# VectorE's order in the retention heads of a decoder layer: the value block's first sum and the sine product trade places

## The chip, the cores and the metric

One core of one Trainium2 chip runs the whole program. The metric is the device time of one execution in microseconds, from first to last instruction of the core, with what lies around them; the median of several runs counts.

## The reference, cut to what matters

The program is one decoder layer in float32 on 8 sequences of 100 tokens (800 columns): retention with 8 heads, cross attention to a context of 722 tokens, a gated feed-forward part, each followed by a sum with its input and a layer norm. The change lies in the retention alone:

```
q, k = rope(x @ Wq), rope(x @ Wk)          # per head 128 wide
v, g = x @ Wv, x @ Wg                      # per head 256 wide
scores = (q * scale) @ k.T * decay         # per batch and head
o = scores @ v
o = o * rsqrt(mean(o*o) + eps) * g_norm_weight * silu(g)
attn = o.reshape(B, T, H * DV) @ Wo
rope(x) = [x1*cos - x2*sin, x2*cos + x1*sin]
```

The inputs are float32, and the outputs keep that precision.

## The kernel before, in words

**Precision by splitting.** Each float32 operand is split into a high part in fp32r, which ScalarE copies, and a low part, which VectorE gets by subtracting the high part from the source. A product is three TensorE passes: high by high, high by low, low by high. So each 128x512 piece of weights costs one ScalarE instruction (`entry_hi`, L1726) and one VectorE subtraction (`entry_lo`, L1993) ahead of TensorE's use. A ring of four pieces holds them: ScalarE may write piece e only when TensorE has finished piece e - 4.

**The heads.** Head 0 and head 7 are written apart. Heads 1 to 6 run the function `head(i)`, once in each engine's program. A head has three blocks: block 0 is query and key, block 1 the two value tiles, block 2 the two gate tiles. A block is computed by a Strassen scheme: seven products p0 to p6 of 12 matmuls each (L2511, L2513, L2515; each 128x400), from four mixed weight pieces (`mix`, L2025) and mixed activations that are kept (SIDE). The sums of products are made by VectorE (`combine`, L2051) out of PSUM in the order u2, u3, c22, c21, c12, with one copy by ScalarE before them (`keep`) and one between (`first_quarter`, L1758). TensorE's product p3 of a block waits for the sum u2 of that block, p5 for u3, p6 for c22, since they write the PSUM banks that these sums read.

**The order of one head on TensorE**: seven products of block 0 (with the transposes of the head before between them), seven of block 1, the output projection of head i - 1 in eight tiles (`project_output`, L2372 to L2374), scores, transposes of the values, seven products of block 2. The eight tiles take turns in two pairs of PSUM banks, so tile n from the third on waits until VectorE has added tile n - 2 to R (`add_output`, L2114): `if n >= 2: pe.wait_ge(r_added, 8 * i + (n - 1 - 8))`.

**The rotation.** Query (n = 0) and key (n = 1) share the two scratch tiles T1 and T2. For each of them VectorE multiplies by the cosine into T1 (`rotate_cos`, L2093) and by the sine into T2 (`rotate_sin`, L2097). GpSimd waits for the sine product and issues two accumulating DMAs that add T2 with its halves exchanged to T1 (L1700), waits until both have landed, and raises `roped` (L1703). ScalarE then makes the high part (`rotated_hi`, L1784), VectorE the low part (`rotated_lo`, L2104), and only then may the cosine product of n = 1 write T1. VectorE's queue is in order: what stands behind `rotated_lo` waits with it.

**Weights.** SyncE loads 1 MB pairs of pieces (L1661). The load of block 2's pair is issued when the low part of block 1's last piece (p6) is made, that of the next head's first pair when the low part of the fourth output piece is made.

Every order here is written out by hand, in `head(i)` of `vector` and of `scalar`; nothing plans it. Lines touched: `head` in `vector` and `head` in `scalar`. Lines of helpers that the steps below pass: `combine` L2051, `mix` L2025, `entry_lo` L1993, `output_lo` L2164, `gated_output` L2174.

Of the kernel before, what the change touches and what calls it, by code (L numbers as in the profile page):

```python
# [1514 lines left out]
def phase_retention(c, nc, sem, before, norm):  # L1515


    with ExitStack() as ctx:
# [186 lines left out]
        def scalar(act):  # L1705
# [30 lines left out]
            def output_entry_hi(i, n):  # L1736
                pair = pair_of(i, 2)
                entry_hi(PER * (i - 1) + OUTPUT_ENTRY + n, raw_quarters(pair)[:, n, :], pair, None)
# [43 lines left out]
            def rotated_hi(i, n):  # L1782
                act.wait_ge(roped, 2 * i + (n + 1))
                act.activation(QK[n][0], T1, ACT.Copy).then_inc(qk_hi, 1)  # L1784
# [81 lines left out]
            def head(i):  # L1866

                if i > 1:
                    product_hi(i, 0, 3)
                    keep(i, 0)  # L1870
                product_hi(i, 0, 4)
                if i == 1:
                    side_hi(4)
                else:
                    act.preload_act_table_set("silu_and_others")
                    gates(i - 1)
                    act.preload_act_table_set("natural_log_exp_and_others")
                product_hi(i, 0, 5)
                product_hi(i, 0, 6)
                if i > 1:  # L1880
                    output_hi(i - 1)
                product_hi(i, 1, 0)
                first_quarter(i, 0)
                if i == 1:
                    output_hi(i - 1)
                product_hi(i, 1, 1)
                product_hi(i, 1, 2)

                product_hi(i, 1, 3)
                keep(i, 1)  # L1890
                product_hi(i, 1, 4)
                product_hi(i, 1, 5)
                product_hi(i, 1, 6)
                output_entry_hi(i, 0)
                rotated_hi(i, 0)
                output_entry_hi(i, 1)
                first_quarter(i, 1)
                output_entry_hi(i, 2)
                output_entry_hi(i, 3)
                rotated_hi(i, 1)  # L1900
                product_hi(i, 2, 0)
                product_hi(i, 2, 1)
                product_hi(i, 2, 2)
                product_hi(i, 2, 3)
                scores_hi(i)
                turned_hi(i)
                keep(i, 2)
                product_hi(i, 2, 4)
                product_hi(i, 2, 5)
                product_hi(i, 2, 6)  # L1910
                token_squares(i, 0)
                if i < STRASSEN:
                    product_hi(i + 1, 0, 0)
                token_squares(i, 1)
                if i < STRASSEN:
                    product_hi(i + 1, 0, 1)
                else:
                    u = U_END_HEAD
                    act.wait_ge(c.raw[(u // 2) % 2], raw_count(u // 2))
                    act.wait_ge(f_done, F_DONE + LAST_ENTRY - 1)  # L1920
                    act.activation(c.WH[:, u % 2, :], raw_unit(c, u), ACT.Copy).then_inc(c.w_hi, 1)
                root(i)
                if i == STRASSEN:
                    act.wait_ge(x_back, X_BACK + 16)
                    act.wait_ge(f_done, F_DONE + LAST_ENTRY)
                    act.activation(operand(0, 1)[0], F1, ACT.Copy).then_inc(t_hi, 1)
                scaled_rows(i)
                if i < STRASSEN:
                    product_hi(i + 1, 0, 2)
# [45 lines left out]
        def vector(dve):  # L1975
# [30 lines left out]
            def mix(i, j, n):  # L2006

                pair, m = pair_of(i, PAIR[j]), block(i, j)
                raw = raw_quarters(pair)
                if n == 0:  # L2010
                    dve.wait_ge(c.raw[pair % 2], raw_count(pair))
                    if m > 0:
                        dve.wait_ge(f_lo, F_LO + entry(i - (j == 0), (j - 1) % 3, 3) + 1)
                    out, x, y, op = S3[:], raw[:, 0, :], raw[:, 2, :], ALU.subtract
                elif n == 1:
                    out, x, y, op = raw[:, 2, :], raw[:, 2, :], raw[:, 3, :], ALU.add
                elif n == 2:
                    dve.wait_ge(f_lo, F_LO + entry(i, j, 0) + 1)
                    out, x, y, op = raw[:, 0, :], raw[:, 2, :], raw[:, 0, :], ALU.subtract
                else:  # L2020
                    dve.wait_ge(f_lo, F_LO + entry(i, j, 4) + 1)
                    out, x, y, op = raw[:, 1, :], raw[:, 1, :], raw[:, 0, :], ALU.subtract
                if n:
                    dve.wait_ge(s_op, S_OP + 4 * m + n)
                dve.tensor_tensor(out, x, y, op).then_inc(s_op, 1)  # L2025
# [178 lines left out]
            def head(i):  # L2204
                if i > 1:
                    combine(i - 1, 2, "c12")
                    product_lo(i, 0, 2)
                    product_lo(i, 0, 3)
                    product_lo(i, 0, 4)
                    mix(i, 0, 3)  # L2210
                    combine(i, 0, "u2")
                    gated_output(i - 1)
                    product_lo(i, 0, 5)
                    combine(i, 0, "u3")
                    combine(i, 0, "c22")
                    mix(i, 1, 0)
                    mix(i, 1, 1)
                    product_lo(i, 0, 6)
                else:
                    combine(i, 0, "u2")  # L2220
                    product_lo(i, 0, 4)
                    mix(i, 0, 3)
                    side_lo(4)
                    product_lo(i, 0, 5)
                    combine(i, 0, "u3")
                    combine(i, 0, "c22")
                    product_lo(i, 0, 6)
                    mix(i, 1, 0)
                    gated_output(i - 1)
                product_lo(i, 1, 0)  # L2230
                if i == 1:
                    mix(i, 1, 1)
                mix(i, 1, 2)
                product_lo(i, 1, 1)
                output_lo(i - 1, 0)
                combine(i, 0, "c21")
                output_lo(i - 1, 1)
                product_lo(i, 1, 2)

                combine(i, 0, "c12")  # L2240
                product_lo(i, 1, 3)
                rotate_cos(i, 0)
                product_lo(i, 1, 4)
                rotate_sin(i, 0)
                mix(i, 1, 3)
                combine(i, 1, "u2")
                product_lo(i, 1, 5)
                combine(i, 1, "u3")
                combine(i, 1, "c22")
                product_lo(i, 1, 6)  # L2250
                output_entry_lo(i, 0)
                rotated_lo(i, 0)
                rotate_cos(i, 1)
                rotate_sin(i, 1)
                output_entry_lo(i, 1)
                combine(i, 1, "c21")
                output_entry_lo(i, 2)
                add_output(0, i)
                combine(i, 1, "c12")

                output_entry_lo(i, 3)
                add_output(1, i)
                mix(i, 2, 0)
                add_output(2, i)
                rotated_lo(i, 1)
                product_lo(i, 2, 0)
                add_output(3, i)
                mix(i, 2, 1)
                add_output(4, i)
                mix(i, 2, 2)  # L2270
                product_lo(i, 2, 1)
                add_output(5, i)
                product_lo(i, 2, 2)
                add_output(6, i)
                add_output(7, i)
                product_lo(i, 2, 3)
                mask_scores(i)
                scores_lo(i)
                turned_low(i)

                product_lo(i, 2, 4)
                combine(i, 2, "u2")
                mix(i, 2, 3)
                product_lo(i, 2, 5)
                product_lo(i, 2, 6)
                combine(i, 2, "u3")
                combine(i, 2, "c22")
                if i < STRASSEN:
                    mix(i + 1, 0, 0)
                    mix(i + 1, 0, 1)  # L2290
                    product_lo(i + 1, 0, 0)
                    mix(i + 1, 0, 2)
                    product_lo(i + 1, 0, 1)
                else:
                    plain_lo(U_END_HEAD)
                combine(i, 2, "c21")
# [2150 lines left out]
```

## Time and profile before

| what | value |
|---|---|
| median of 3 runs | 2631.72 us (2630.65 to 2632.12) |
| profiled execution, its own time | 2630.63 us |
| its span, first to last instruction | 2628.8 us |
| TensorE busy (matmul) | 2593.5 us, 99% |
| VectorE busy | 1814.5 us, 69% |
| ScalarE busy | 1197.4 us, 46% |
| heads 1 to 6 | about 548 to 988 us of the span |

The heads 2 to 6 are 72.5 us each. A matmul's busy time is longer than the distance to the next one (0.34 against 0.18 us), since they are pipelined; so a hole in TensorE's work is read from the starts of neighbouring matmuls. The granted TensorE clock was full throughout (0.999 over the span).

### The profile page before, as it was taken

To read this page: it belongs to the slowest core of one execution; us is meant where nothing else is said; L and a number is where in the kernel's file an instruction comes from. 1 tells how busy PE (TensorE), PEld (TensorE's weight loads), DVE (VectorE), ACT (ScalarE), POOL (GpSimd) and SP (SyncE) were. 2 spreads that over 40 slices of the span, in tenths; PEclk is the share of its full clock that TensorE was granted. 3 is DMA by queue.
4 is the path that set the end of the run, shared out by engine and by line. 5 is a ranking of instruction groups with operands and counts; after the bars stand their busy time and mean duration, and the time that the engine had idled before them with its cause. 6 is when DMAs were issued, how large, how long until landed. Compare 5 with 4: busy or idle time off the path is not lost.

```text
span 2628.8 us, 41662 instructions
## 1 busy us (share of the span) xinstructions
PE 2593.5 (99%) x16328; PEld 2456.2 (93%) x16328; DVE 1814.5 (69%) x2506; ACT 1197.4 (46%) x2043; POOL 20.7 (1%) x33
## 2 busy tenths in 40 slices
PE   9999999999999999999999999999999999999998
PEld 9999999989999998898889999889998999999997
DVE  7777776677777774867788888736973763763766
ACT  6555555554444443344466666522531431431441
POOL 0000000000000000000000000000000000000000
PEclk9999999999999999999999999999999999999999
DMA  5444445422222231144256666421121121211121
GB/s 197 160 145 161 149 135 180 146 71 63 61 72 62 78 90 51 63 105 92 77 143 175 174 168 166 107 72 57 48 81 48 65 81 49 81 65 65 65 80 51
DMA packets 138188, 262.68 MB, mean 100 GB/s; under 512 B 25012, under 2 KB 98220, under 8 KB 125100
## 3 DMA queue, kind: packets, MB, share of 16 engines
q1 hardware_dynamic: 136108, 255.53, 30.9%
q0 software_dynamic: 1920, 4.92, 1.1%
q8 instruction: 113, 1.85, 0.3%
q14 instruction: 47, 0.39, 0.0%
HBM read 198.24 MB, written 57.26 MB: 97 GB/s over the span
## 4 chain that ended last, share of the span: by engine, by line
PE 91%; DVE 6%; issue 2%; ACT 1%; DMA 0%; DVEq 0%; SPq 0%; ACTq 0%
PE PS L3666 6%; PE PS L3664 6%; PE PS L3668 6%; PE PS L3137 5%; PE PS L135 4%; PE PS L133 4%; PE PS L134 4%; PE PS L3150 3%; PE PS L1167 3%; PE PS L1169 3%; PE PS L1171 3%; PE PS L1130 3%; PE PS L1132 3%; PE PS L1134 3%; PE PS L3702 3%; PE PS L3701 3%
## 5 line engine op out<-in xcount | busy, mean ns | idle before, releaser
L3807 ACT ACTIVATE WH<-RAW 128x512 fp32r<-128x512 f32 x180 | 113.4, 631 | 222.2 <-PE PS L3668 119.8
L133 PE MATMUL PS<-XH,WH 128*128 128x512 f32 (+1 forms) x592 | 204.2, 345 | 1.0 <-DVE WL L99 1.0
L135 PE MATMUL PS<-XH,WL 128*128 128x512 f32 (+1 forms) x592 | 204.4, 345 | 0.0
L4048 DVE TENSOR_TENSOR WL<-RAW,WH 128x512 fp32r<-128x512 f32 x196 | 134.7, 688 | 58.5 <-ACT WH L3807 55.2
L134 PE MATMUL PS<-XL,WH 128*128 128x512 f32 (+1 forms) x496 | 170.1, 343 | 0.0
L3666 PE MATMUL PS<-XL,WH 128*128 128x400 f32 x480 | 166.0, 346 | 0.0
L3664 PE MATMUL PS<-XH,WH 128*128 128x400 f32 x480 | 164.8, 343 | 0.8 <-issue 0.6
L3668 PE MATMUL PS<-XH,WL 128*128 128x400 f32 x480 | 165.0, 344 | 0.0
L3309 DVE TENSOR_TENSOR XL<-PS,XH 128x400 fp32r<-128x400 f32 (+2 forms) x224 | 122.6, 571 | 56.5 <-ACT XH L3242 51.6
L3242 ACT ACTIVATE XH<-PS 128x400 fp32r<-128x400 f32 (+2 forms) x224 | 106.3, 507 | 96.1 <-PE PS L3150 96.0
L1726 ACT ACTIVATE WH<-RAW 128x512 fp32r<-128x512 f32 x132 | 81.5, 632 | 117.6 <-DVE RAW L2025 66.5
L3702 PE MATMUL PS<-t_ROOM,WL 128*128 128x512 f32 (+1 forms) x384 | 132.5, 345 | 0.0
L3701 PE MATMUL PS<-t_ROOM,WH 128*128 128x512 f32 (+1 forms) x384 | 131.7, 343 | 0.0
L3700 PE MATMUL PS<-t_ROOM,WH 128*128 128x512 f32 (+1 forms) x384 | 131.6, 343 | 0.0
L3290 DVE TENSOR_REDUCE a_LOW<-PS 100x1 f32<-100x824 f32 x128 | 129.7, 1014 | 2.6
L3664 PE MATMUL PS<-t_ROOM,WH 128*128 128x400 f32 x360 | 124.4, 346 | 0.3 <-issue 0.3
L1167 PE MATMUL PS<-WALL,WH 128*128 128x256 f32 x448 | 124.4, 278 | 0.0
L1169 PE MATMUL PS<-WALL,WL 128*128 128x256 f32 x448 | 124.3, 277 | 0.0
L1171 PE MATMUL PS<-WALL,WH 128*128 128x256 f32 x448 | 124.2, 277 | 0.0
L3666 PE MATMUL PS<-t_ROOM,WH 128*128 128x400 f32 x360 | 124.1, 345 | 0.0
L3668 PE MATMUL PS<-t_ROOM,WL 128*128 128x400 f32 x360 | 124.0, 344 | 0.0
L133 PEld LDWEIGHTS PS<-XH,WH 128*128 128x128 f32 x592 | 111.2, 188 | 12.7 <-issue 1.2
(535 smaller groups left out, 8162.8 us busy)
## 6 DMA issues: line engine op xcount, KB each, us to landing
RAW<-weights_dram SPq DMA_DIRECT2D x100, 1024.0 KB, 4.9
values_scratch<-VS SPq DMA_DIRECT2D x44, 512.0 KB
a_KHL<-keys_scratch SPq DMA_DIRECT2D x32, 411.0 KB, 5.1
RAW<-context_dram SPq DMA_DIRECT2D x6, 2048.0 KB, 8.7
XH<-values_scratch SPq DMA_DIRECT2D x16, 640.0 KB
XL<-values_scratch SPq DMA_DIRECT2D x16, 640.0 KB
R<-context_dram SPq DMA_DIRECT2D x4, 2048.0 KB, 9.2
keys_scratch<-KS SPq DMA_DIRECT2D x16, 512.0 KB, 3.8
```

The lines of the kernel that those rows point to most:

```text
L133: pe.matmul(out, wh, xh[:, k, cols], start=(k == 0), stop=False)
L134: pe.matmul(out, wh, xl[:, k, cols], start=False, stop=False)
L135: mm = pe.matmul(out, wl, xh[:, k, cols], start=False, stop=(k == KT - 1))
L1167: pe.matmul(out, hi[:, k, cols], wh, start=(opens and t + k == 0), stop=False, skip_group_check=True)
L1169: pe.matmul(out, lo[:, k, cols], wh, start=False, stop=False, skip_group_check=True)
L1171: mm = pe.matmul(out, hi[:, k, cols], wl, start=False, stop=(k == QUAD - 1), skip_group_check=True)
L3664: pe.matmul(out, wh, high[:, k, :], start=(OPENS[p] and k == 0), stop=False, skip_group_check=True)
L3666: pe.matmul(out, wh, low[:, k, :], start=False, stop=False, skip_group_check=True)
L3668: mm = pe.matmul(out, wl, high[:, k, :], start=False, stop=(k == QUAD - 1), skip_group_check=True)
L3701: pe.matmul(out, wh, HL[:, k, cols], start=False, stop=False)
L3702: mm = pe.matmul(out, wl, HH[:, k, cols], start=False, stop=(i == KT - 1))
L4048: dve.tensor_tensor(ring[1][:, e % RING, :], src, ring[0][:, e % RING, :].bitcast(F32), ALU.subtract).then_inc(f_lo, 1)
```

## The change

VectorE's order in heads 1 to 6 is changed, and one pair on ScalarE. No instruction is added or removed. On VectorE:

- The value block's first sum, `combine(i, 1, "u2")`, goes ahead of the low part of p4, the cosine product, the low part of p5 and the sine product. Before, it stood behind cosine, low part of p4, sine and `mix(i, 1, 3)`.
- `rotate_sin(i, 0)` goes behind `mix(i, 1, 3)` and the low part of p5; `rotate_cos(i, 0)` behind the low part of p4.
- `output_lo(i - 1, 1)` goes from ahead of p2's low part to behind u2; `combine(i, 0, "c21")` goes one place up.
- The second output piece's low part goes ahead of `rotated_lo(i, 0)`. On ScalarE its high part goes ahead of `rotated_hi(i, 0)`.
- In head 1 alone, `mix(1, 1, 1)` goes ahead of `gated_output(0)`.

```
                 product_hi(i, 1, 6)
                 output_entry_hi(i, 0)
+                output_entry_hi(i, 1)
                 rotated_hi(i, 0)
-                output_entry_hi(i, 1)
                 first_quarter(i, 1)
...
                     mix(i, 1, 0)
+                    mix(i, 1, 1)
                     gated_output(i - 1)
                 product_lo(i, 1, 0)
-                if i == 1:
-                    mix(i, 1, 1)
                 mix(i, 1, 2)
                 product_lo(i, 1, 1)
+                combine(i, 0, "c21")
                 output_lo(i - 1, 0)
-                combine(i, 0, "c21")
-                output_lo(i - 1, 1)
                 product_lo(i, 1, 2)
 
                 combine(i, 0, "c12")
                 product_lo(i, 1, 3)
+                combine(i, 1, "u2")
+                output_lo(i - 1, 1)
+                product_lo(i, 1, 4)
                 rotate_cos(i, 0)
-                product_lo(i, 1, 4)
+                mix(i, 1, 3)
+                product_lo(i, 1, 5)
                 rotate_sin(i, 0)
-                mix(i, 1, 3)
-                combine(i, 1, "u2")
-                product_lo(i, 1, 5)
                 combine(i, 1, "u3")
                 combine(i, 1, "c22")
                 product_lo(i, 1, 6)
                 output_entry_lo(i, 0)
+                output_entry_lo(i, 1)
                 rotated_lo(i, 0)
                 rotate_cos(i, 1)
                 rotate_sin(i, 1)
-                output_entry_lo(i, 1)
                 combine(i, 1, "c21")
                 output_entry_lo(i, 2)
                 add_output(0, i)
```

## Rows read from the trace of the kernel before

**Rows 1.** The page, part 1: busy time, share of the span, instructions.

```profile
PE 2593.5 (99%) x16328; PEld 2456.2 (93%) x16328; DVE 1814.5 (69%) x2506; ACT 1197.4 (46%) x2043; POOL 20.7 (1%) x33
```

**Rows 2.** TensorE's waits in heads 1 to 6: us in total, times, longest.

```profile
PE PS L2511 <- DVE W L2051: 5.9, 6, 2.1
PE PS L2511 <- DVE WL L1993: 0.8, 2, 0.4
```

**Rows 3.** Timeline of TensorE, head 5: start, us, engine, line, tiles, idle before.

```profile
861.61 0.34 PE L2515 MATMUL PS<-SIDE,WL 128*128 128x400 f32 x1
...
863.79 0.34 PE L2515 MATMUL PS<-SIDE,WL 128*128 128x400 f32 x1
...
864.90 0.45 PE L2511 MATMUL PS<-SIDE,WH 128*128 128x400 f32 x1 [0.76 <-DVE W L2051]
...
865.18 0.34 PE L2513 MATMUL PS<-SIDE,WH 128*128 128x400 f32 x1
...
873.77 0.39 PE L2372 MATMUL PS<-VHL,WH 128*128 128x512 f32 x1
...
878.12 0.40 PE L2372 MATMUL PS<-VHL,WH 128*128 128x512 f32 x1
```

**Rows 4.** Timeline of VectorE, head 5.

```profile
858.68 0.98 DVE L2164 TENSOR_TENSOR VHL<-G,VHL 128x800 fp32r<-128x800 f32 x1
...
861.27 0.98 DVE L2093 TENSOR_TENSOR T<-QKR,COS 128x800 f32<-128x800 f32 x1
862.17 0.68 DVE L1993 TENSOR_TENSOR WL<-RAW,WH 128x512 fp32r<-128x512 f32 x1
862.77 0.98 DVE L2097 SCALAR_TENSOR_TENSOR T<-QKR,SIN 128x800 f32<-128x800 f32 x1
...
864.28 0.56 DVE L2051 TENSOR_TENSOR W<-U,PS 128x400 f32<-128x400 f32 x1
...
868.55 1.29 DVE L1993 TENSOR_TENSOR WL<-RAW,WH 128x512 fp32r<-128x512 f32 x2
869.76 0.99 DVE L2104 TENSOR_TENSOR QK<-T,QK 128x800 fp32r<-128x800 f32 x1
870.78 0.99 DVE L2093 TENSOR_TENSOR T<-QKR,COS 128x800 f32<-128x800 f32 x1
871.69 0.98 DVE L2097 SCALAR_TENSOR_TENSOR T<-QKR,SIN 128x800 f32<-128x800 f32 x1
...
873.67 0.68 DVE L1993 TENSOR_TENSOR WL<-RAW,WH 128x512 fp32r<-128x512 f32 x1
876.15 0.99 DVE L2114 TENSOR_TENSOR R<-R,PS 128x800 f32<-128x800 f32 x1 [1.79 <-PE PS L2374]
```

**Rows 5.** Timeline of ScalarE: `rotated_hi`, heads 5 (twice), 6 and 2.

```profile
868.65 0.87 ACT L1784 ACTIVATE QK<-T 128x800 fp32r<-128x800 f32 x1 [0.62 <-POOLq L1703]
...
877.78 0.87 ACT L1784 ACTIVATE QK<-T 128x800 fp32r<-128x800 f32 x1 [3.18 <-POOLq L1703]
...
943.03 0.88 ACT L1784 ACTIVATE QK<-T 128x800 fp32r<-128x800 f32 x1 [2.52 <-POOLq L1703]
...
662.62 0.87 ACT L1784 ACTIVATE QK<-T 128x800 fp32r<-128x800 f32 x1 [5.46 <-POOLq L1703]
```

**Rows 6.** Timeline of GpSimd, head 6: the second DMA of a rotation.

```profile
939.88 0.83 POOL L1700 DMA_DIRECT2D T<-T  x1 [2.54 <-issue]
```

**Rows 7.** Windows of head 5; the last two columns are DMA share and GB/s.

```profile
865.40:868.60 3.20, 3.20 (x19) 3.20 (x18) 1.15 (x4) 0.63 (x1) 0.29 (x1) 1.00 0.77 128
868.60:870.20 1.60, 1.60 (x11) 1.60 (x10) 1.60 (x4) 1.50 (x3) 0.00 (x0) 1.00 0.00 0
870.20:873.60 3.40, 3.40 (x21) 3.40 (x20) 3.37 (x5) 1.03 (x3) 0.63 (x2) 1.00 0.96 306
```

**Rows 8.** Timeline of head 1: VectorE's low part of p0, TensorE's p3.

```profile
563.93 0.68 DVE L1993 TENSOR_TENSOR WL<-RAW,WH 128x512 fp32r<-128x512 f32 x1
...
574.97 0.45 PE L2511 MATMUL PS<-SIDE,WH 128*128 128x400 f32 x1 [2.12 <-DVE W L2051]
```

More of the change, by code:

```diff
@@ L1894, in head @@
                 output_entry_hi(i, 0)
+                output_entry_hi(i, 1)
                 rotated_hi(i, 0)
-                output_entry_hi(i, 1)
                 first_quarter(i, 1)
@@ L2228, in head @@
                     mix(i, 1, 0)
+                    mix(i, 1, 1)
                     gated_output(i - 1)
                 product_lo(i, 1, 0)
-                if i == 1:
-                    mix(i, 1, 1)
                 mix(i, 1, 2)
                 product_lo(i, 1, 1)
+                combine(i, 0, "c21")
                 output_lo(i - 1, 0)
-                combine(i, 0, "c21")
-                output_lo(i - 1, 1)
                 product_lo(i, 1, 2)
@@ L2241, in head @@
                 product_lo(i, 1, 3)
+                combine(i, 1, "u2")
+                output_lo(i - 1, 1)
+                product_lo(i, 1, 4)
                 rotate_cos(i, 0)
-                product_lo(i, 1, 4)
+                mix(i, 1, 3)
+                product_lo(i, 1, 5)
                 rotate_sin(i, 0)
-                mix(i, 1, 3)
-                combine(i, 1, "u2")
-                product_lo(i, 1, 5)
                 combine(i, 1, "u3")
@@ L2251, in head @@
                 output_entry_lo(i, 0)
+                output_entry_lo(i, 1)
                 rotated_lo(i, 0)
@@ L2254, in head @@
                 rotate_sin(i, 1)
-                output_entry_lo(i, 1)
                 combine(i, 1, "c21")
```

## The prediction

> **What bounds the kernel now.** I read the page first: TensorE is busy 99% of the span [rows 1], so only a hole in TensorE's work can be won, and any new hole is paid in full. Then TensorE's waits over heads 1 to 6: six waits of block 1's product p3 for VectorE's sum into W, which is u2, 5.9 us together, the longest 2.1; and two small ones for low parts, 0.8 us, both in head 1 [rows 2]. Then the timeline at one of the holes. In head 5 the last matmul of p2 starts at 863.79; matmuls follow each other every 0.18, so p3 was due at 863.97 and started at 864.90, 0.93 late; the one behind it came 0.28 later instead of 0.18. **One hole costs 1.04** [rows 3], more than its 0.76 of idle time, because busy times overlap. VectorE's timeline says why: u2 ran at 864.28 behind cosine, low part and sine [rows 4], although the product it reads (p1) had ended at 861.61 + 0.34 = 861.95 [rows 3].
>
> **What the change removes.** The new order starts u2 at 861.98 (0.03 after p1's end; VectorE has done all ahead of it by 861.27 - 0.90 = 860.4, since one `output_lo` no longer stands there, and idles until then). It ends at 862.54, 1.4 before p3 is due. The hole goes in heads 2 to 6: 5 x 1.04 = 5.2. In head 1 p3 came 2.28 + 0.1 late (574.97, idle 2.12 + 0.16 of overlap) [rows 8], and the two small waits cost 0.6 and 0.7 in the same way: 3.7. There the change puts `mix(1, 1, 1)` and its wait for the mix before it (0.72) ahead of p0's low part (563.93) [rows 8]; that piece gets late by as much and p0 with it, 0.7. Of the three holes 3.0 are regained. **Regained: 8.2.** The low parts of p4, p5, p6 and the sums u3, c22 stay 0.8 us or more ahead of their products, so no stall at those places takes over.
>
> **What it moves: the sine product, and all that hangs on it.** One VectorE instruction behind another starts 0.08 before the profiled end of the first. From u2 on: u2 0.48, `output_lo` 0.90, low part 0.60, cosine 0.90, mix 0.61 (864.28 - 862.77 less the sine's 0.90), low part 0.60, then the sine, 0.98 [rows 4]. It ends at 861.98 + 4.09 + 0.98 = 867.05. Before, it ended at 863.75. **3.3 us later**, while TensorE is 1.04 earlier. GpSimd's two DMAs start with it. From the sine's end to `rotated_hi` head 5 needed 868.65 - 863.75 = 4.9 [rows 4, 5]; call this L1. Then comes a chain on VectorE in which nothing can be overtaken: ScalarE's high part to VectorE's start 0.90, `rotated_lo` 1.02 (869.76 to 870.78), cosine 0.91, then sine, c21 and one low part 1.98 (871.69 to 873.67, the same three lengths), `add_output(0)` 0.99 [rows 4, 5]: 5.8 in all. So the first add ends at 867.05 + 4.9 + 5.8 = 877.75.
>
> When is it due? TensorE's third output tile waits for it. That tile started at 878.12, without the hole it is due at 877.08 [rows 3]. Before, the add began the moment its tile was ready (876.15, idle 1.79 ahead) and left 1 us of room; now VectorE is late by 0.7, plus 0.1 for the restart. **A hole at the third tile of size L1 - 4.2 + 0.1.** Over the six heads the time from sine to `rotated_hi` was 5.3, 4.9, 5.9, 5.3, 4.9, 6.8 (head 5 and head 6 are in [rows 5]; head 6 shows 1.9 more idle time, 2.52 against 0.62, because GpSimd issued its second DMA only after 2.54 of "issue" [rows 6]). Heads 2 to 6: 0.8 + 1.8 + 1.2 + 0.8 + 2.7 = 7.3. In head 1 the sine is 0.4 later still against p3, as VectorE comes late out of the gate: 1.7. Together 9.0.
>
> **The second rotation** hangs behind the first. Let X be the start of the key's sine product. The first add ends at X + 2.97, the third tile starts with it, the sixth 6.68 later, at X + 9.65; that tile waits for `add_output(3)`, which stands behind `rotated_lo(i, 1)` in VectorE's queue. That add ends at X + 0.98 + L2 + 0.90 + 1.02 + 0.60 + 0.99. So a second hole opens once L2 is over 5.1. In head 5 L2 was 877.78 - 872.67 = 5.1, and most heads are like it; head 2 had 2.28 more (idle 5.46 against 3.18) [rows 5]. That makes 2.4 in head 2 and 0.1 to 0.3 in the others: 3.0.
>
> ScalarE's swapped pair costs nothing: the high part of the second output piece is ready once p4 is done (868.5), and `rotated_hi` now comes only after 871.9. Without it that piece would be stuck behind the rotation. The first quarter of block 1 waits behind `rotated_hi` until 872.8; its readers stand behind the whole projection in TensorE's order. The weight load for block 2 leaves 0.4 earlier and lands as early; its first user, `mix(i, 2, 0)`, stands behind the second add.
>
> **So far 12.0 lost against 8.2 regained: +3.8.**
>
> **The transfers now meet.** In head 5 the rotation's two DMAs kept the DMA engines 77% busy from 865.4 to 868.6, nothing ran for 1.6 us, and block 2's weights took 96% of them from 870.2 to 873.6 [rows 7]. The weight load is released by p6's low part (868.55 [rows 4]), 1.65 ahead of its traffic; in the new order this piece comes at 868.15, so the weights come from 869.8 to 873.2. The rotation's traffic shifts with the sine to 868.7 to 871.9, of which some 1.3 us of work is left once the weights are in full flow. No row shows such an overlap. Ends: nothing (what is queued first goes first), or all weights first: 1.3 of work from 873.2 on lands at 874.5 instead of 871.9, 2.6. I take 1.0, nearer the lower end: what is left, shared evenly, doubles, and the first packets still find room. Six heads: 6.0. The second rotation touches the next head's load only with its tail, 0.2 in five heads, and 0.8 in head 2, where its second DMA is late: 1.8. The Trainium skill ("DMA: Bandwidth & Descriptors", "Queues, rings and completion order") says that each DMA engine goes round between the queues it has work for, a whole packet at a time; by that rule the delay would be real and could come near the upper end. The profile so far only shows that the two together ask for more than the engines have, 0.77 and 0.96.
>
> **Sum:** 2630.63 - 8.2 + 9.0 + 3.0 + 7.8 = 2642.2 against the profiled run's own time, which is 1.1 below the median of the runs; I give **2642**. A measurement of this kernel can tell about 0.2%, 5.3 us, from no change.
>
> **Rivals.**
> (a) *The transfers don't hurt each other.* Then +3.8: 2634.5 to 2635.6, no measurable change. For it: the second rotation DMA is queued before the weights. Against: both ask for full engines. 0.24.
> (b) *The hole is simply removed*, faster. Its place is the third output tile; it decides at L1 = 4.2 and L2 = 5.1. Were every rotation under these, only the regained 8.2 would stay: 2622.4. Against: the shortest of the six L1 was 4.9, and two waits of GpSimd for "issue" are of its own queue and stay. For it: in the trace before, the first add waited for TensorE and not the other way round. 0.04.
> (c) *The weights go first.* The rotation waits for the whole burst: 2.6 instead of 1.0 in six heads, +9.6: 2652. 0.10.
> (d) *The order does nothing*, as VectorE's u2 is held by ScalarE's `keep` copy instead. But `keep` waits for p0 alone, a product of 2.2 us before p1, and u2 can't be ahead of p1 anyway. 0.01.
> My forecast has the rest, 0.61.
>
> **Range and chances.** Low end 2633.5 (case a, with head 3's 5.9 taken as an accident), high end 2648 (2.0 per head for the overlap); this leaves out b and most of c. Faster by over 0.2% is b, 0.04. Within 0.2%, up to 2637.0, is a and d, 0.25. Slower is my forecast and c, 0.71.
>
> **What would show it.** In the new trace: no wait of L2511 for W; instead waits of L2372 (the projection's first matmul of a tile) for VectorE's R, L2114, at the third tile in every head, some 0.7 to 3.7 each, and at the sixth in head 2 at least; in head 1 one small wait of p0 for a low part. `rotated_hi` should show 4 us or more of idle time before it, and VectorE some 2 to 4 us idle ahead of `rotated_lo`. A sine-to-`rotated_hi` time of 5.9 instead of 4.9 in head 5 proves the overlap; 4.9 proves (a). If L2372 waits for nothing, the whole argument is wrong.

## The result, and the profile after

| | before | after |
|---|---|---|
| median | 2631.47 us (4 runs) | 2661.98 us (2660.09 to 2663.35, 4 runs) |
| ratio | | 1.0116, interval 1.0098 to 1.0133 |
| profiled execution, span | 2628.8 us | 2661.0 us |
| mean granted TensorE clock | 0.999 | 0.994 |

The change makes the kernel 30.5 us slower. I had forecast slower, but by a third of that. One of the four runs of the kernel with one weight load cut took 3634.63 us and one run of the kernel before, measured with it, 3167.21 us; these two slow runs are left out of what follows.

The page of the changed kernel, part 1, has VectorE and ScalarE as they were. TensorE is busy for a smaller share of a longer span, yet for 11.4 us more in all, with the same instructions [rows 1]:

```profile
PE 2604.9 (98%) x16328; PEld 2466.2 (93%) x16328; DVE 1814.3 (68%) x2506; ACT 1197.4 (45%) x2043; POOL 20.7 (1%) x33
```

TensorE's waits in heads 1 to 6 of the changed kernel (us in total, times, longest; lines of `head` are one lower than before):

```profile
PE PS L2371 <- DVE R L2114: 26.8, 8, 6.3
PE PS L2510 <- DVE WL L1993: 0.5, 1, 0.5
```

The wait for W, 5.9 us in six pieces [rows 2], is gone. In its place stand eight waits of the output projection for VectorE's sum into R, four and a half times as much. Six of them are the third output tile's, one per head, two the sixth's, in heads 2 and 3. The small wait left is p0 of head 1.

Head 5 of the changed kernel, VectorE's timeline (start, us, line, tiles, idle before); it answers to [rows 4]:

```profile
886.40 0.98 DVE L2097 SCALAR_TENSOR_TENSOR T<-QKR,SIN 128x800 f32<-128x800 f32 x1
...
888.46 1.89 DVE L1993 TENSOR_TENSOR WL<-RAW,WH 128x512 fp32r<-128x512 f32 x3
896.62 0.99 DVE L2104 TENSOR_TENSOR QK<-T,QK 128x800 fp32r<-128x800 f32 x1 [6.27 <-ACT QK L1784]
897.64 0.99 DVE L2093 TENSOR_TENSOR T<-QKR,COS 128x800 f32<-128x800 f32 x1
898.55 0.98 DVE L2097 SCALAR_TENSOR_TENSOR T<-QKR,SIN 128x800 f32<-128x800 f32 x1
...
899.93 0.69 DVE L1993 TENSOR_TENSOR WL<-RAW,WH 128x512 fp32r<-128x512 f32 x1
900.54 0.98 DVE L2114 TENSOR_TENSOR R<-R,PS 128x800 f32<-128x800 f32 x1
```

ScalarE's high part of the rotated query, and TensorE's third output tile behind the last of these rows, the add:

```profile
895.71 0.88 ACT L1784 ACTIVATE QK<-T 128x800 fp32r<-128x800 f32 x1 [6.22 <-POOLq L1703]
```

```profile
901.66 0.47 PE L2371 MATMUL PS<-VHL,WH 128*128 128x512 f32 x1 [4.10 <-DVE R L2114]
```

Read from top to bottom, this is the chain of the prediction: the sine ends at 887.38, VectorE finishes two sums and three low parts, is idle for 6.3 us until the rotated query is there, then runs `rotated_lo`, cosine, sine, c21, one low part and the add without a gap, and TensorE starts 0.14 after the add's end. From `rotated_hi` to the add's end it took 901.52 - 895.71 = 5.81, the 5.8 that I had summed. What is not as predicted is the first step: from the sine's end to `rotated_hi` passed 8.3 us, not 4.9 nor 5.9.

Windows of the same stretch show why (last three columns: granted clock, DMA share, GB/s). The rotation's traffic, before alone at 0.77 [rows 7], and the weights', before alone at 0.96, now share one stretch:

```profile
888.90:890.10 1.20, 1.20 (x8) 1.20 (x7) 1.20 (x3) 0.58 (x1) 0.42 (x1) 1.00 0.98 163
890.10:892.90 2.80, 2.80 (x17) 2.80 (x17) 0.24 (x1) 0.00 (x0) 0.00 (x0) 1.00 0.94 200
892.90:895.70 2.80, 2.80 (x17) 2.46 (x16) 0.00 (x0) 0.00 (x0) 0.00 (x0) 1.00 0.66 251
```

And there is a second thing that the prediction had no term for: the granted clock. In head 2, behind the third tile's hole (2.73 us idle), TensorE went at its lower level, 1.2 GHz, for 3.4 us. Two windows of equal length, the first at 0.50 and the second at 1.00 (the column before the DMA share), show 12 matmuls against 18, and the first of them were 0.43 us apart instead of 0.23:

```profile
667.40:670.60 3.20, 3.20 (x12) 2.81 (x11) 1.75 (x3) 0.00 (x0) 0.82 (x1) 0.50 0.60 154
670.80:674.00 3.20, 3.20 (x18) 2.75 (x17) 0.83 (x1) 0.00 (x0) 0.00 (x0) 1.00 0.81 222
```

The clock records of the trace have six such stretches in the heads of the changed kernel, 27.2 us together, and none in those of the kernel before. TensorE's 11.4 us of extra busy time fit this: the same matmuls take longer there.

**Where the 32.2 us of span went** (2661.0 against 2628.8). I add up TensorE's holes in the heads as the step between two matmuls' starts less the usual 0.18. Before: 8.0 us. After: 28.4 (third tiles, heads 1 to 6: 3.5, 2.8, 2.6, 4.9, 4.2, 6.4; sixth tiles 2.8 and 0.5; p0 of head 1 0.7). That is 20.4 more. The remaining 11.8 us are close to half of the half-clock time in which TensorE worked: 27.2 less about 4 that lay inside holes, halved, is 11.6.

### The profile page after: what moved, and what is told of

It reads as the page before. It is cut to its first block, busy times and chain, and to the rows that moved or that the text cites. A ratio compares the mean times of both kernels' runs of the same rounds, so it can differ in the third digit from the quotient of the medians.

```text
span 2661.0 us, 41662 instructions
## 1 busy us (share of the span) xinstructions
PE 2604.9 (98%) x16328; PEld 2466.2 (93%) x16328; DVE 1814.3 (68%) x2506; ACT 1197.4 (45%) x2043; POOL 20.7 (1%) x33
## 4 chain that ended last, share of the span: by engine, by line
PE 89%; DVE 5%; DMA 2%; issue 2%; ACT 1%; POOL 0%; DVEq 0%; SPq 0%; POOLq 0%; ACTq 0%
PE PS L3665 6%; PE PS L3663 6%; PE PS L3667 6%; PE PS L3136 5%; PE PS L135 4%; PE PS L133 4%; PE PS L134 4%; PE PS L3149 3%; PE PS L1167 3%; PE PS L1169 3%; PE PS L1171 3%; PE PS L1130 3%; PE PS L1132 3%; PE PS L1134 3%; PE PS L3701 3%; PE PS L3700 3%
## 5 line engine op out<-in xcount | busy, mean ns | idle before, releaser
L133 PEld LDWEIGHTS PS<-XH,WH 128*128 128x128 f32 x592 | 111.3, 188 | 12.7 <-issue 1.2
```

The lines of the kernel that those rows point to most:

```text
L133: pe.matmul(out, wh, xh[:, k, cols], start=(k == 0), stop=False)
```

## The experiments

Theory after the result: (1) the sine product's new place makes the first add late; (2) it also pushes the rotation's DMAs under block 2's weight load, and the key's under the next head's; (3) the holes that come of it are long enough for the granted clock to fall. Rivals: another part of the change costs (ScalarE's swap, the late `output_lo`); the long rotations have another cause than the weights; the clock's fall is in the records but costs little.

### The sum alone

The kernel before, with u2 moved between the query's cosine and sine. So that the sine comes no later, the low part of p4 goes behind it.

```
                 rotate_cos(i, 0)
-                product_lo(i, 1, 4)
+                combine(i, 1, "u2")
                 rotate_sin(i, 0)
+                product_lo(i, 1, 4)
                 mix(i, 1, 3)
-                combine(i, 1, "u2")
                 product_lo(i, 1, 5)
```

> The kernel before, with the value block's first sum alone moved: it stands between the query's cosine and sine products. The sine ends at most 0.1 us later than before in heads 2 to 6. Theory (the sine's lateness makes the loss, the sum's early place only removes holes): no wait of L2511 for W in heads 2 to 6, no new wait at the output tiles but for at most 1 us in head 6, the granted clock full in the heads; 5 holes of 1.04 us and about 2.2 us of head 1's go, so 6.5 to 7.5 us less than before, about 2624.5. Rival (the sum's early place costs by itself, or the holes are filled by other waits): the time of before or above it.

Measured: 2624.19 us (2623.72 to 2624.68), ratio 0.9973, interval 0.9963 to 0.9984. In heads 1 to 6 only head 1's two small waits are left, the same as in the second line of [rows 2].

Here VectorE has the cosine at 856.76, u2 at 857.66 and the sine at 858.14: u2 follows the cosine at once, since by then p1 is done, and the sine stands 1.38 behind the cosine, not 1.50 as before [rows 4]. So what the change was good for can be had without its price. The holes fell by 6.9 us and the time by 7.0.

### The sine put back

The changed kernel, with cosine and sine of the query straight behind u2.

```
                 combine(i, 1, "u2")
-                output_lo(i - 1, 1)
-                product_lo(i, 1, 4)
                 rotate_cos(i, 0)
+                rotate_sin(i, 0)
+                product_lo(i, 1, 4)
+                output_lo(i - 1, 1)
                 mix(i, 1, 3)
                 product_lo(i, 1, 5)
-                rotate_sin(i, 0)
```

> The changed kernel, with cosine and sine of the query put straight behind the sum u2, ahead of the low part of p4 and of output_lo: the sine ends 2.7 us earlier than in the changed kernel, 0.6 us later than before. All else of the change stays, ScalarE's swap too. Theory (the place of the sine is the whole loss): the transfers hardly meet the weights, query rotations of 4.9 to 6.8 us, no hole at the third tile but in head 6 (up to 1 us), full clock, 2623 to 2627. Rival (other parts of the change cost too, ScalarE's swap or the late output_lo): 2632 or more.

Measured: 2629.33 us (2627.41 to 2632.12), ratio 0.9995, interval 0.9985 to 1.0004. So 32.7 us of the changed kernel go with the sine's place, and the kernel ends 2 us above what I had expected. Nearly all of the rest has one address, the key's rotation of head 2 (head 6's third tile has another hole, of 0.5). Its ScalarE row and the sixth tile behind it:

```profile
662.88 0.87 ACT L1784 ACTIVATE QK<-T 128x800 fp32r<-128x800 f32 x1 [9.42 <-POOLq L1703]
```

```profile
666.46 0.66 PE L2371 MATMUL PS<-VHL,WH 128*128 128x512 f32 x1 [2.79 <-DVE R L2114]
666.92 0.63 PE L2372 MATMUL PS<-VHL,WH 128*128 128x512 f32 x1
```

That rotation took 9.9 us, a hole of 2.9 came of it, and the matmuls behind it are at half clock again (0.63 long instead of 0.40). It is the rotation whose second DMA GpSimd issues late, which led to the next run.

### More room for GpSimd's descriptors

```
-    nc = bacc.Bacc("TRN2", ..., dynamic_dma_scratch_size=1024)
+    nc = bacc.Bacc("TRN2", ..., dynamic_dma_scratch_size=2048)
```

> The changed kernel, with the room for GpSimd's DMA descriptors doubled from 1024 to 2048. Theory (the two waits of GpSimd for issue, in head 2's second and head 6's first rotation, are a full ring of descriptors that waits for the DMA before): both go or move to other heads; head 6's query rotation falls from 10.5 to about 8, and head 2's key rotation from 9.6 to about 7; 3 to 6 us less than the changed kernel, 2656 to 2659. Rival (the wait has another cause): both stay, and the time is that of the changed kernel, 2662.

Measured on the changed kernel: 2652.3 us (2650.05 to 2654.56), 9.7 less, more than the 3 to 6 expected. GpSimd's timeline shows both DMAs issued together where one had waited 2.5 us for "issue" [rows 6]; for head 2's key and head 6's query:

```profile
663.17 1.64 POOL L1700 DMA_DIRECT2D T<-T  x2 [9.30 <-DVE T L2097]
...
958.92 1.64 POOL L1700 DMA_DIRECT2D T<-T  x2 [63.57 <-DVE T L2097]
```

Their rotations fell from 9.6 to 6.8 and from 10.5 to 7.2. The wait was a matter of descriptor room: in every kernel with 1024 the 8th and the 22nd of these 24 DMAs waited until the one before had landed, and in every kernel with 2048 none did. The profiled execution was the slowest of the four, 8.3 us below that of the changed kernel; of these, 6.2 are holes and the rest goes with 20.4 instead of 27.2 us at half clock. I had priced the holes alone. Not all of it is the two late DMAs either: head 4, in which no DMA waited for issue in either kernel, has its query's rotation at 7.1 instead of 9.1 us and 1.4 us less of holes, for a reason that no run shows.

The same room with the sine put back:

> The run with cosine and sine put back (2629.3), with the room for GpSimd's DMA descriptors doubled. Theory (what it had left over were the two rotations whose second DMA waits for issue: a hole of 2.9 us and half-clock behind it in head 2, 0.5 us in head 6): both holes and the drop go, 2623.5 to 2625.5. Rival (the rest comes from another part of the change, ScalarE's swap or the late output_lo): 2628 or more.

Measured: 2622.63 us (2622.32 to 2623.0), ratio 0.9967, interval 0.9955 to 0.9979. One wait of TensorE is left in the heads, p0 of head 1, 0.5 us as in the changed kernel.

This is the fastest kernel of the study. It carries everything of the change but the place of the query's cosine and sine (and has `output_lo` one place further back), so neither the late `output_lo` nor, in this order, ScalarE's swap costs anything that shows.

And with the sum alone moved:

> The run with the sum alone moved (2624.2), with the doubled room. It has no hole at the output tiles, so the shorter rotations save nothing on TensorE's path: 2623.5 to 2625. Rival (the wait for issue costs somewhere that the waits of TensorE don't show): 2621 or less.

Measured: 2623.69 us (2623.26 to 2623.86), as expected: 0.5 below the run without it. Head 6's rotation got shorter there too, 7.0 to 5.1, and since no tile waited for it, next to nothing came of it.

### Taking the weights' traffic away

The changed kernel, with the load of the gate block's weights (heads 1 to 6) cut to 32 columns. Its place, its wait and its semaphore stay; the gate products of these heads then work on what lies in the buffer.

```
                 sp.wait_ge(f_lo, F_LO + PER * (i - 1) + 14)
-                load_pair(pair_of(i, 3))
+                last = pair_of(i, 3)
+                sp.dma_start(c.RAW[:, last % 2, 0:32], c.weights[last][:, 0:32]
+                             ).then_inc(c.raw[last % 2], 16)
```

> The changed kernel, with the gate block's weight load in heads 1 to 6 cut from 1 MB to 32 columns, so that its place and semaphore stay and its traffic goes (the gate products of these heads then use what lies in the buffer). Theory (the rotation's DMAs share the engines with this load): sine to rotated_hi falls from 6.7 to 10.5 us back to 4.9 to 6.8 for the query; the holes at the third output tile fall to 0.7 to 2.8 us, the clock drops at one hole at most, and the time is 2635 to 2642. Rival (the lateness of the sine or a slower DMA for another reason makes the long rotations): they stay above 6.5 us and the time stays above 2655.

Measured: 2644.05 us (2643.62 to 2646.16, three runs), ratio 1.0053, interval 1.0035 to 1.0072; 17.9 us less than the changed kernel and 2 above my span. The query's rotations fell to 5.3, 5.2, 5.2, 5.1, 6.2, 6.8, from 7.3, 7.0, 6.7, 9.1, 8.3, 10.5, with the sine as late as in the changed kernel. So the length comes from the weights' traffic and not from the sine's lateness. What I had underrated is the key: its rotations still met the next head's load, 9.9 us in head 2, and made four holes at the sixth tile, up to 4.5 us idle.

With the next head's load (heads 2 to 6) cut as well:

> The changed kernel, with both weight loads that meet a rotation (gate block, and query and key of the next head for heads 2 to 6) cut to 32 columns; those products use what lies in the buffers. This is the prediction's case without any overlap. By its terms: query rotations 4.9 to 6.8 us, key rotations 5.1 and 7.4 in head 2, holes of 12 to 13 us in all instead of 28.4, the clock dropping once at most, behind head 6's or head 2's hole: 2635 to 2638. Rival (my terms of the schedule are wrong too, not only the overlap and the clock): 2642 or more.

Measured: 2637.34 us (2635.73 to 2640.16), ratio 1.0024, interval 1.0013 to 1.0034. Query rotations 5.3, 5.0, 5.2, 5.2, 5.5, 6.8, key rotations 5.0 to 5.2 but for 7.1 in head 2 and 6.6 in head 4. Head 4's query, which took 9.1 us in the changed kernel, takes 5.2.

TensorE's holes are 12.4 us; my terms without overlap were 12.0 and head 1's 0.7. This tests how I had worked out the schedule, and it holds. The clock fell twice, 6.8 us together. Half of that, 3.4, more than covers the distance from my +3.8 to the measured +6.2.

### Releasing the load later

```
-                sp.wait_ge(f_lo, F_LO + PER * (i - 1) + 14)
+                sp.wait_ge(f_lo, F_LO + PER * (i - 1) + 16)
                 load_pair(pair_of(i, 3))
```

> The changed kernel, with the load of block 2's weights released two pieces later (when the second output piece's low part is made), so that it leaves about 1.2 us later and meets only the last 0.8 us of the query's rotation. The key's rotation still meets the next head's load. Overlap theory: query rotations 5.3 to 6 us instead of 6.7 to 10.5 (head 6 about 8), holes at the third tile about 1 to 2 us, at most two or three clock drops, 2642 to 2652. Rival (the long rotations come from their own lateness): they stay near 7 us or more and the time stays at 2658 or more.

Measured: 2651.32 us (2646.71 to 2652.68), ratio 1.0077, interval 1.006 to 1.0094. Shifted by 1.2 us, the same megabyte cost the rotations of heads 1 to 5 only what I had expected (5.8, 5.0, 5.7, 5.6, 5.7); head 6's, whose second DMA comes late, still met it in full, 9.5. The key's of head 2 still met the next head's load, 9.9. The traffic's timing is what counts, and 10.7 us can be had by moving a load back by one wait value.

### What a hole costs by itself

To price the clock without any DMA, I took the kernel with the sum alone moved and let VectorE make the third output piece's low part five or eight times over before it counts as made, 0.72 us each, so that the first add is late. The eightfold kernel's edit (the other has 5 for 8 in both places):

```
+                e = PER * (i - 1) + OUTPUT_ENTRY + 2
+                dve.wait_ge(f_hi, F_HI + e + 1)
+                for n in range(8):
+                    dve.tensor_tensor(ring[1][:, slot(e), :], raw_quarters(pair_of(i, 2))[:, 2, :],
+                                      ring[0][:, slot(e), :].bitcast(F32), ALU.subtract).then_inc(c.made, 1)
+                    dve.wait_ge(c.made, 4 + 8 * (i - 1) + n + 1)
                 output_entry_lo(i, 2)
```

> The kernel of the run with the sum alone moved (2624.2), with the low part of the third output piece made five times over ahead of the first add, 0.72 us each, so that TensorE has a hole of about 1.7 us at the third tile of each head while no transfer is moved into another. Clock theory: holes this small leave the granted clock full and cost their own length, 6 x 1.7: 2633 to 2636. Rival (a hole costs more than its length whatever its size): 2640 or more.

> The same with eight repetitions, holes of about 3.9 us, 23 us in all. Clock theory: the granted clock falls to 1.2 GHz for about 3.4 us or more behind each hole, 1.7 us more per head, 10 us in all: 2656 to 2661. Rival (the fall of the clock shows in the records but costs little): 2646 to 2649.

Measured: 2644.26 us (2641.61 to 2646.09) and 2665.95 us (2665.44 to 2668.07). TensorE's waits of the two:

```profile
PE PS L2378 <- DVE R L2114: 14.0, 6, 3.5
```

```profile
PE PS L2378 <- DVE R L2114: 27.0, 6, 5.7
```

The first missed: the holes were not 1.7 in every head but 3.1, 1.8, 2.5, 1.9, 1.8, 3.7, because heads 3 and 6, whose query rotations took 5.8 and 7.0 us, and head 1, where the sine is later against p3, had less room to start with. The clock fell at three of them, the three longest, and not at the others, and with that the time came out 8 us above my span. The second's holes were 3.9 to 5.8 and its time 5 us above my span: the clock fell at all six, in four of them for 6.8 us. Windows of head 4 at either level, 16 matmuls against 33:

```profile
824.80:830.30 5.50, 5.50 (x16) 4.63 (x17) 3.56 (x6) 0.00 (x0) 0.00 (x0) 0.50 0.60 192
831.00:836.50 5.50, 5.50 (x33) 4.94 (x32) 3.88 (x6) 0.69 (x2) 0.00 (x0) 1.00 0.01 6
```

Nine of the profiled executions side by side, against the kernel with the sum alone moved (span 2622.4, holes 1.1, clock full); "left" is the growth of the span less the growth of the holes:

| kernel | span | holes | at half clock | left |
|---|---|---|---|---|
| before | 2628.8 | 8.0 | 0 | -0.5 |
| sine put back | 2626.3 | 4.1 | 3.4 | 0.9 |
| both loads cut | 2637.1 | 12.4 | 6.8 | 3.4 |
| small holes | 2641.6 | 15.7 | 10.2 | 4.6 |
| one load cut | 2641.8 | 17.0 | 6.8 | 3.5 |
| load later | 2644.9 | 20.2 | 6.8 | 3.4 |
| more room | 2652.7 | 22.2 | 20.4 | 9.2 |
| changed | 2661.0 | 28.4 | 27.2 | 11.3 |
| large holes | 2663.3 | 28.8 | 34.0 | 13.2 |

The last column follows the one before it, at 0.4 to 0.5 per us in all but the sine put back, where it is 0.3 of a small number. Half of the time at half clock that lies outside the holes meets it within 1 us in every row, whatever made the holes. In the three kernels that are not in the table the clock did not fall in the heads: the swap alone has 0.1 left, and the two with the doubled room and no lateness -1.0 and -1.5; so up to 1.5 us of a span have another source, which no run shows.

### ScalarE's swap alone

The kernel before, with the second output piece moved ahead of `rotated_hi` on ScalarE and of `rotated_lo` on VectorE.

> The kernel before, with the second output piece alone moved ahead of rotated_hi on ScalarE and ahead of rotated_lo on VectorE. Both engines have idle time there (ScalarE 0.6 us, VectorE 1.8 us before the first add) and the six holes of the sum u2 stay: the time of before within 1 us. Rival (the swap itself delays the key's rotation into the next load): 2634 or more.

Measured: 2634.51 us (2631.58 to 2637.16), ratio 1.0013, interval 1.0003 to 1.0022. I expected no change, and it costs some 3 us in the median, as the rival said. ScalarE's timeline of head 5 shows a step that I had left out:

```profile
870.49 0.63 ACT L1726 ACTIVATE WH<-RAW 128x512 fp32r<-128x512 f32 x1 [1.55 <-PE PS L2515]
871.03 0.86 ACT L1784 ACTIVATE QK<-T 128x800 fp32r<-128x800 f32 x1
```

The piece's high part waits for TensorE (p4), and `rotated_hi` now stands behind it: 6.3 us from the sine in heads 1 to 5, although the DMAs had landed after 5.0 to 5.2. So the key's sine stands 10.2 us behind the query's in head 5, not 8.9. The profiled execution was the fastest (2631.58) and shows one hole for it, 0.26 us at the sixth tile of head 2. The executions scatter over 5.6 us; the five over 2635 have a mean granted clock of 0.997 or 0.998, the five below 0.998 or 0.999, so holes with a fall of the clock are likely in them. No profile shows which, and the way from the swap to the 3 us stays open. In the changed kernel `rotated_hi` comes at 895.71, long behind that piece's high part (888.85), so the swap can't hold it there.

## Why the prediction was wrong

**Right.** What bounds the kernel, the 8.2 us regained (no wait for W, head 1's new wait of p0, 0.7 as worked out; the kernel with the sine put back and the doubled room, which has hardly more than this term, gained 8.7), the place of the new holes, and the size that each has for a given rotation: L1 - 4.2 + 0.1 gives 2.9, 2.6, 5.0, 4.2, 6.4 for heads 2 to 6 and the trace has 2.8, 2.6, 4.9, 4.2, 6.4. Case (a), no overlap, was priced at +3.8 and 12.7 us of holes; with the traffic taken away the chip gave +6.2 and 12.4.

**Wrong in size: the overlap.** "I take 1.0, nearer the lower end." The six query rotations grew from 33.1 to 48.8 us, 2.6 each in the mean. That is the upper end that I had worked out myself for all weights going first. But it is no bound: by head they grew 1.9, 2.1, 0.8, 3.8, 3.4 and 3.7, and that the mean falls on it is in part luck. The first DMA of a rotation landed as before, 3.4 after the sine in head 5; the second, issued 0.5 later, landed at 8.3 instead of 4.8.

What failed is "what is left, shared evenly, doubles". The DMA view of head 5, 890.5 to 893.5, has (queue, packets, MB, share) the weights first and the rotation second:

```profile
q1 hardware_dynamic: 66, 0.54, 66.9%
q0 software_dynamic: 58, 0.17, 31.5%
```

The queues take turns packet by packet, but the packets are unequal: 3200 bytes in 0.26 us for the rotation, 8192 bytes in 0.31 us for the weights; the rotation's last two start 0.57 apart, which is one of each. So the rotation got about a quarter of the bytes, not half. And a DMA has landed only when the slowest of its sixteen shares has (each closes with a packet of 4 bytes): in head 5 fifteen were through 6.3 us after the sine, when 0.6 of the megabyte had passed, and the last at 7.9, when nearly all had. In every head at least 650 KB of the 1 MB of weights passed before the query's rotation was through. The Trainium skill ("DMA: Bandwidth & Descriptors", "Queues, rings and completion order") has each DMA engine drain a whole packet of one queue before it turns to another; I had named the rule as pointing to the upper end and then let the milder estimate stand against it. The turns in the trace agree with the rule.

The key's overlap was also larger than the 0.2 and 0.8 I gave: 0.5, 2.2, 0.5, 1.3, 0.6, 0.8. Of the second holes I had 4.8 us; the trace has 3.3. The likely reason is that a third tile at half clock also gives VectorE time; no run separates it.

**Missing: the clock.** My sum said that any new hole is paid in full and had no term beyond that. A hole is paid in full and more: 11.8 of the 32.2 us are TensorE at 1.2 GHz behind the holes, more than half of the 20 us by which the forecast fell short. The page of before had shown the clock full throughout and I took it as given. A kernel with holes of 0.9 and one of 2.3 us had no fall, so nothing in the trace of before told where it begins. But a case in which it falls should have stood among the rivals; with it the range would have reached above 2648.

Together: rival (c) for the overlap, 2652, and 11.8 for the clock, less the 1.5 that the second holes were short of my 4.8, give 2662, where 2662 was measured. I gave (c) 0.10, and (c) by itself, without the clock, would have missed by 10 us.

## What to carry to other kernels

When an instruction that starts a DMA moves later, follow the transfer's traffic as well as its landing: write down what else is on the DMA engines in its new stretch, and where both would fill them, price the small transfer as if it waited for the big one (here it was through only when at least 650 KB of the 1 MB had passed). On an engine that is busy 99% of the time, a hole of two or three microseconds can cost half as much again in granted clock, so besides the sum of the holes that a change may open look at each one that is that long. And where a sum is wanted earlier, move the sum, not what stood ahead of it: moving this one sum gained 7 us where the whole reordering lost 30.

## What the runs showed of the hardware that I had not expected

- A rotation's second DMA (200 KB, like the first) landed 8.3 us after the sine instead of 4.8 when a 1 MB load was released 1.8 us after the sine, and at 5.6 in the same head with the load released 1.2 us later still. The packets of both queues took turns one by one, 3200 bytes against 8192.
- The clock's fall does not go by the length of the one hole alone: behind 1.75 us of idle TensorE (head 2, both loads cut) it fell, behind 2.46 us (head 3 of the changed kernel) it did not. A fall lasted 3.4 or 6.8 us.
- With 1024 of descriptor room the 8th and the 22nd of GpSimd's 24 DMAs waited 2.5 us for the one before to land; with 2048 none did, and the changed kernel was 9.7 us faster.
